# Context and attention in one block: the attention's tiles over the context's, its first loads issued during the eighth context block

## The chip, the core and the metric

The kernel runs on one core of a Trainium2 chip. The time is the device time of one execution in microseconds (us); a kernel's time is the median of its runs. Engines are named as in the profile: PE is TensorE, ACT ScalarE, DVE VectorE, POOL GpSimd, and SP is SyncE, which here only issues DMA transfers.

## The reference, cut to what matters

Four cross-attention layers on the same stream `x` (8 x 512 tokens x 512 channels) against one context (8 x 77 x 1024). Layers 0 and 2 are of kind A, 1 and 3 of kind B.

```python
# layers 0 and 2 (16 heads of 64, own K/V heads, bias on a few context columns)
q = x @ Wq;  k = ctx @ Wk;  v = ctx @ Wv
logits = einsum('bhqd,bhkd->bhqk', q, k) * 64 ** -0.5 + col_bias
x = softmax(logits) @ v  -> (B, 512, 1024) @ Wo + bo + x
# layers 1 and 3 (16 heads of 32, 4 K/V heads, rms norm of x)
xn = x * rsqrt(mean(x * x) + eps) * norm_w
q = xn @ wq;  k = ctx @ wk;  v = ctx @ wv
x = x + softmax(q k / sqrt(32)) @ v @ wo
```

Keys and values depend on the context alone, so they can be computed for all four layers ahead of the attention. Each float32 product is formed from a high and a low part in three matmul passes (`three_passes`, lines 228 to 232).

## The kernel before

The program is two hardware blocks, one after the other, in each of which every engine has its own hand-written instruction list. At the end of a block all five engines meet in a barrier.

**The context block** (`context_block`) projects the context with nine pairs of weight blocks, j = 0 to 8 (`NJ`): eight pairs for layers 0 and 2, one for layers 1 and 3 together. For each j, PE makes the keys (four banks, 96 matmuls of 308 columns) and then the values (five groups of rows r = 0 to 4, banks 4 to 7 and again 4, 24 matmuls of 256 columns each). ACT copies each bank's high part out and DVE subtracts it to get the low part (`drain_keys`, `drain_values`); both also split the next weights (`split_weights`). SP issues for each j: the two loads of the weights of j + 1 into `kvw_raw` (line 329), four stores of `k_out` to the scratch `k_scr` (line 340) and two of `v_out` to `v_scr` (lines 345 and 347).

In the ninth pair (j = 8) there are no further context weights. In their place SP loads the attention's first batch of x into `kvw_raw` slot 0 (line 331), half of the first query weights `wqA` into slot 1 (line 333), and, after x has been split (`late_lo` at least 1), the other half into slot 0 again (line 335). ACT splits x (`split_late(0)`, line 389) as its last work of j = 7, ahead of all of its work for j = 8. It splits the two weight halves between the drains of keys and of values of j = 8. PE's values r = 4 use bank 4 a second time, and so wait until DVE has drained r = 0 (the wait on `v_lo` in `values`). SP's last instruction in the block waits until every store has landed.

**The attention block** (`attention_block`) runs 128 units (4 layers, 8 batches, 4 head groups) in a software pipeline of steps: queries of the next unit, scores of this one, transposes of the one before, values of the one two back, projections. At its start POOL clears `keys_s` and `vals_s`, and SP issues the first loads, in this order: keys of unit 0 (2 transfers), two pieces of weights into `stage`, three of x into `x_front`, keys of unit 1 (2), values of units 0 and 1 (16 small transfers, line 663), four of x into `x_back`. After them SP follows the steps. All transfers of the kernel are issued by SP, on one queue.

The tiles of the two blocks take SBUF in turn; what lasts over both (`w_s`, `x_s` and some constants) is in `Lasting`.

Of the kernel before, what the change touches and what calls it, by code (L numbers as in the profile page):

```python
# [13 lines left out]

# [12 lines left out]
P = 128  # L27
# [226 lines left out]
def context_block(nc, lasting, ctxT, kvw, k_scr, v_scr, k1_scr, v1_scr, x_in, wqA, boA, normB, masks, tokens,  # L254
# [5 lines left out]
    with ExitStack() as ctx:  # L260
# [6 lines left out]
        ctx_raw = sb("ctx_raw", [P, KC, ROWS], F32)  # L267
        ctx_s = sb("ctx_s", [P, 2, KC, ROWS], F32R)
        w_raw = sb("kvw_raw", [P, 2, PART], F32)
        k_out = sb("k_out", [P, 2, 2, ROWS], F32R)  # L270
        v_out = sb("v_out", [P, len(VROWS), 2, BLK], F32R)
        banks = [ctx.enter_context(nc.psum_tensor(f"ctx_bank{i}", [P, 512], F32)) for i in range(8)]

        w_A, x_s, ident, mean_w, mhalf = lasting.w_s, lasting.x_s, lasting.ident, lasting.mean_w, lasting.mhalf
        bias_s, bo, nw = lasting.bias_s, lasting.bo, lasting.nw
        w_s = w_A[:, 2:4]
        tok_i = sb("tok_i", [P, 8], I32)
        tok_f = sb("tok_f", [P, 2, 8], F32)

        mask_b = sb("mask_b", [P, 2, TILES], F32)  # L280
        iota_t = ctx_raw[:, 2, 0:CTX]
        cmp_t = [ctx_raw[:, 2, CTX * (1 + n):CTX * (2 + n)] for n in range(3)]

        ctx_loaded = [sem(f"ctx_loaded{n}") for n in range(KC // 2)]
        first_loaded = [sem(f"first_loaded{n}") for n in range(KC // 2)]
        first_hi, first_lo = sem("first_hi"), sem("first_lo")
        w_loaded = [sem("kw_loaded"), sem("vw_loaded")]
        ctx_hi, ctx_lo = sem("ctx_hi"), sem("ctx_lo")
        w_hi, w_lo = [sem("kw_hi"), sem("vw_hi")], [sem("kw_lo"), sem("vw_lo")]
        k_mm, v_mm = sem("k_mm"), sem("v_mm")  # L290
        k_hi, k_lo, v_hi, v_lo = sem("k_hi"), sem("k_lo"), sem("v_hi"), sem("v_lo")
        k_stored, v_stored = sem("k_stored"), sem("v_stored")
        consts, cleared, setup_loaded, chain = map(sem, ("consts", "setup_cleared", "setup_loaded", "dve_chain"))
        late_loaded = [sem("x_first"), sem("wq_first"), sem("wq_second")]
        late_hi, late_lo = sem("late_hi"), sem("late_lo")
        NV = len(VROWS)
        FULL = sum(r == P for r in VROWS)

        def late_parts(n):
            if n == 0:  # L300
                return [x_s[:, 0, h].rearrange("p k n -> p (k n)") for h in range(2)]
            return [w_A[:, n - 1, h] for h in range(2)]

        def keys_stored(j):
            return 64 * j

        def vals_stored(j):
            return 32 * j

        block = ctx.enter_context(nc.Block())  # L310

        @block.sync
        def _(sp):
            for k in range(0, KC, 2):
                sp.dma_start(w_raw[:, 0, BLK * k:BLK * (k + 2)], kvw[0][:, BLK * k:BLK * (k + 2)]).then_inc(first_loaded[k // 2], 16)
                sp.dma_start(ctx_raw[:, k:k + 2], ctxT[:, k:k + 2]).then_inc(ctx_loaded[k // 2], 16)
            sp.dma_start(w_raw[:, 1], kvw[1]).then_inc(w_loaded[1], 16)
            sp.dma_start(mask_b[:, :, :], masks).then_inc(setup_loaded, 16)
            sp.dma_start(tok_i[:, :], tokens[:, ::token_words].partition_broadcast(P)).then_inc(setup_loaded, 16)
            sp.dma_start(bo[:, :, :], boA).then_inc(setup_loaded, 16)  # L320
            sp.dma_start(nw[:, :, :], normB).then_inc(setup_loaded, 16)
            for j in range(NJ):
                for slot in range(2):
                    if j == 0 and slot == 0:
                        sp.wait_ge(first_lo, KC // 2)
                    else:
                        sp.wait_ge(w_lo[slot], j + slot)
                    if j + 1 < NJ:
                        sp.dma_start(w_raw[:, slot], kvw[2 * j + 2 + slot]).then_inc(w_loaded[slot], 16)
                    elif slot == 0:  # L330
                        sp.dma_start(w_raw[:, 0], x_in[0].rearrange("p k n -> p (k n)")).then_inc(late_loaded[0], 16)
                    else:
                        sp.dma_start(w_raw[:, 1], wqA[0, 0]).then_inc(late_loaded[1], 16)
                        sp.wait_ge(late_lo, 1)
                        sp.dma_start(w_raw[:, 0], wqA[0, 1]).then_inc(late_loaded[2], 16)
# [23 lines left out]
        def _(act):  # L359
# [11 lines left out]
            def drain_keys(n, j):  # L371
                m, h = n // 2, n % 2
                act.wait_ge(k_mm, 4 * j + n + 1)
                if n == 0 and j:
                    act.wait_ge(k_stored, keys_stored(j))
# [951 lines left out]
```

## Time and profile before

| | us |
|---|---|
| median of 3 runs (2130.8 to 2134.89) | 2132.19 |
| the profiled execution, whole | 2131.65 |
| its span in the trace | 2129.7 |
| PE busy | 2080.0 (98%) |
| DVE busy | 1361.5 (64%) |
| ACT busy | 927.0 (44%) |
| POOL busy | 690.4 (32%) |

A row of instructions has the start and the duration, the engine, the line, the operation, out<-in and how many were merged, and in brackets how long the engine had been idle and what ended that. SPq rows are DMA issues: their duration is that of issuing, and the landing of the data is shown apart. In a row of stretches, "PEclk" is the granted TensorE clock as a share of full speed (1.00 is the 2.4 GHz level, 0.50 the 1.2 GHz level), "DMA share" the mean busy share of the 16 DMA engines and "GB/s" what they moved. The share can come out a little over 1, as whole packets are counted where they start.

### The profile page before, as it was taken

The page shows a single profiled execution, that of the slowest core. Times are in us where ns is not written, and L with a number is a line of the kernel's source. Part 1 is how long each engine was busy: PE and PEld are TensorE (multiplying, and loading weights), DVE is VectorE, ACT ScalarE, POOL GpSimd, SP SyncE. Part 2 cuts the span into 40 slices and gives each one's busy share as a digit, 9 for nine tenths or more (in the row PEclk, how much of TensorE's full clock was granted, in tenths as well). Part 3 has the DMA queues.
Part 4 walks back from the last instruction along what each step waited for, and adds up shares of the span by engine and source line. Part 5 has one row for each costly group of instructions (what it writes and reads, how often), then busy time and mean ns, then how long its engine had stood idle before and what let it go on. Part 6 is the DMA issues. An engine that isn't in the chain of part 4 may idle for free.

```text
span 2129.7 us, 31554 instructions
## 1 busy us (share of the span) xinstructions
PE 2080.0 (98%) x11674; PEld 1795.4 (84%) x11674; DVE 1361.5 (64%) x2344; ACT 927.0 (44%) x1750; POOL 690.4 (32%) x646
## 2 busy tenths in 40 slices
PE   8999999999999998999999999999999989999998
PEld 8999978888888887788888888888888877888886
DVE  5333355765576556688888675557655765888885
ACT  3222243543354334555555453335433543555552
POOL 0000043312231245465454431223122434554441
PEclk9999999999999999999999999999999999999999
DMA  7777842222222222343333332212221222233322
GB/s 213 173 158 157 179 120 74 67 62 74 54 65 63 77 60 72 85 110 100 86 95 92 102 90 67 73 55 65 63 76 51 70 72 80 67 94 88 87 71 81
DMA packets 260729, 191.02 MB, mean 90 GB/s; under 512 B 195842, under 2 KB 198306, under 8 KB 258018
## 3 DMA queue, kind: packets, MB, share of 16 engines
q1 hardware_dynamic: 260578, 189.02, 34.0%
q8 instruction: 93, 1.52, 0.3%
q14 instruction: 58, 0.48, 0.1%
HBM read 132.66 MB, written 56.26 MB: 89 GB/s over the span
## 4 chain that ended last, share of the span: by engine, by line
PE 38%; issue 31%; POOL 12%; DVE 4%; ACT 1%; SPq 1%; DMA 0%; POOLq 0%; ACTq 0%; DVEq 0%
POOL prob L1197 6%; PE acc_bank L804 6%; PE acc_bank L230 4%; PE acc_bank L232 4%; PE acc_bank L231 4%; PE t_bank L787 4%; PE q_bank L769 3%; PE q_bank L773 3%; PE q_bank L771 3%; POOL x_s L1172 3%; POOL rest L1205 2%; PE s_bank L230 2%; PE s_bank L232 2%; PE s_bank L231 1%; DVE pT_s L1077 1%
## 5 line engine op out<-in xcount | busy, mean ns | idle before, releaser
L1197 POOL TENSOR_TENSOR prob<-prob,rinv 128x1232 f32<-128x1232 f32 x128 | 288.3, 2252 | 1034.9 <-DVE rinv L1092 1034.9
L804 PE MATMUL acc_bank<-pT_s,vals_s 128*128 128x512 f32 x1152 | 369.7, 417 | 0.0
L1055 DVE TENSOR_REDUCE mx<-s_bank 128x4 f32<-128x308 f32 x512 | 243.4, 475 | 187.9 <-PE s_bank L735 117.5
L969 ACT ACTIVATE q_s<-q_bank 128x512 fp32r<-128x512 f32 x192 | 114.8, 598 | 528.7 <-PE q_bank L773 523.6
L769 PE MATMUL q_bank<-x_s,w_s 128*128 128x512 f32 x768 | 320.5, 417 | 4.0 <-POOL w_s L1190 4.0
L773 PE MATMUL q_bank<-x_s,w_s 128*128 128x512 f32 x768 | 314.6, 410 | 0.0
L771 PE MATMUL q_bank<-x_s,w_s 128*128 128x512 f32 x768 | 314.1, 409 | 0.0
L230 PE MATMUL acc_bank<-o_s,w_s 128*128 128x512 f32 x752 | 304.4, 405 | 3.0 <-DVE o_s L1083 3.0
L232 PE MATMUL acc_bank<-o_s,w_s 128*128 128x512 f32 x752 | 298.0, 396 | 0.0
L231 PE MATMUL acc_bank<-o_s,w_s 128*128 128x512 f32 x752 | 297.6, 396 | 0.0
L960 ACT ACTIVATE prob<-prob,rstd 128x308 f32<-128x308 f32 x256 | 140.0, 552 | 288.4 <-DVE prob L1059 260.6
L1059 DVE TENSOR_TENSOR prob<-s_bank,mx 128x308 f32<-128x308 f32 x512 | 244.9, 478 | 26.8 <-DVE mx L1055 0.5
L804 PEld LDWEIGHTS acc_bank<-pT_s,vals_s 128*128 128x128 f32 x1152 | 214.5, 189 | 39.5
L1077 DVE TENSOR_TENSOR pT_s<-t_bank,pT_s 128x512 fp32r<-128x512 f32 x256 | 175.6, 686 | 89.1 <-ACT pT_s L974 89.1
L974 ACT ACTIVATE pT_s<-t_bank 128x512 fp32r<-128x512 f32 x384 | 222.1, 594 | 23.8 <-PE t_bank L787 23.8
L1106 DVE SCALAR_TENSOR_TENSOR x_back<-acc_bank,bo,x_back 128x512 f32<-128x512 f32 x64 | 48.0, 750 | 248.7 <-PE acc_bank L232 248.6
L1089 DVE TENSOR_REDUCE sums<-prob 128x16 f32<-128x1232 f32 x128 | 183.2, 1431 | 3.6 <-ACT prob L952 1.6
L230 PEld LDWEIGHTS acc_bank<-o_s,w_s 128*128 128x128 f32 x752 | 141.6, 188 | 35.7 <-DVE o_s L1083 4.8
L232 PEld LDWEIGHTS acc_bank<-o_s,w_s 128*128 128x128 f32 x752 | 141.6, 188 | 34.3
L231 PEld LDWEIGHTS acc_bank<-o_s,w_s 128*128 128x128 f32 x752 | 142.0, 189 | 31.2
L773 PEld LDWEIGHTS q_bank<-x_s,w_s 128*128 128x128 f32 x768 | 146.1, 190 | 22.8
L769 PEld LDWEIGHTS q_bank<-x_s,w_s 128*128 128x128 f32 x768 | 146.6, 191 | 19.6 <-POOL w_s L1190 4.3
(105 smaller groups left out, 4086.0 us busy)
## 6 DMA issues: line engine op xcount, KB each, us to landing
stream<-x_back SPq DMA_DIRECT2D x128, 256.0 KB, 2.6
x_front<-stream SPq DMA_DIRECT2D x96, 256.0 KB, 3.3
x_back<-stream SPq DMA_DIRECT2D x96, 256.0 KB, 3.9
kvw_raw<-kvw SPq DMA_DIRECT2D x17, 1024.0 KB, 8.6
k_scr<-k_out SPq DMA_DIRECT2D x36, 308.0 KB, 8.4
keys_s<-k_scr SPq DMA_DIRECT2D x128, 77.0 KB, 2.5
v_scr<-v_out SPq DMA_DIRECT2D x8, 1024.0 KB
x_back<-x_in SPq DMA_DIRECT2D x32, 256.0 KB, 4.1
```

The lines of the kernel that those rows point to most:

```text
L230: pe.matmul(out, weights[0], moving[0], start=start, stop=False)
L231: pe.matmul(out, weights[0], moving[1], start=False, stop=False)
L232: return pe.matmul(out, weights[1], moving[0], start=False, stop=stop)
L769: pe.matmul(out, w[0], x_now[0], start=k == 0, stop=False)
L771: pe.matmul(out, w[0], x_now[1], start=False, stop=False)
L773: mm = pe.matmul(out, w[1], x_now[0], start=False, stop=k == XC - 1)
L804: mm = pe.matmul(out, w, pT_s[:, part], start=i == mine[0] and part == 2 * n and w is v[0], stop=i == mine[-1] and w is terms[-1][0] and p ...
L974: act.activation(pT_s[:, 2 * n], t_bank[(3 * u + n) % 2][:, :], ACT.Copy).then_inc(t_hi, 1)
L1055: dve.tensor_reduce(top, scored, AX_X, ALU.max).then_inc(s_max, 1)
L1059: dve.tensor_tensor(prob[:, slot, t].rearrange("q (h n) -> q h n", h=GH), scored, top.unsqueeze(2).broadcast_to([P, GH, CTX]), ALU.subtrac ...
L1077: dve.tensor_tensor(pT_s[:, 2 * n + 1], t_bank[(3 * u + n) % 2][:, :], pT_s[:, 2 * n].bitcast(F32), ALU.subtract).then_inc(t_lo, 1)
L1197: pool.tensor_tensor(view, view, rinv[:, slot].unsqueeze(2).broadcast_to([P, TILES * GH, CTX]), ALU.mult).then_inc(p_norm, 1)
```

## The change

There is one block. `context_part` holds what was `context_block`: it sets up its tiles, gives back their SBUF and PSUM, and returns its five engine lists as functions (`sync`, `scalar`, `vector`, `gpsimd`, `tensor`). `whole_block` is the old `attention_block`, and each of its engines runs the context's list and then its own, with no barrier between. Its tiles lie over the context's: `vals_s`, `keys_s`, `x_front` and the small tiles over `ctx_raw`; `o_s`, `xsq`, `x_power` and `rest` over `ctx_s`; `q_s` over `kvw_raw`; `prob` over `k_out`; `pT_s` over `v_out`; `x_back` and `stage` over the small setup tiles and on free space. Waits on semaphores take the barrier's place.

The first loads become a function `begin()`, which SP calls at j = 7, the eighth pair, after the weight loads of that pair and before the stores of its keys and values. The order in `begin` is new too.

```diff
+    def sync(sp, begin):
...
+                if j + 1 < NJ:
+                    sp.dma_start(w_raw[:, slot], kvw[2 * j + 2 + slot]).then_inc(w_loaded[slot], 16)
...
+            if j == NJ - 2:
+                begin()
+            for m in range(2):
+                sp.wait_ge(k_lo, 4 * j + 2 * m + 2)
...
-            sp.wait_ge(k_stored, keys_stored(NJ))
-            sp.wait_ge(v_stored, vals_stored(NJ - 1) + 48 * PAIRS)
...
+    return Context(sync, scalar, vector, gpsimd, tensor, late_lo, k_lo, 4 * NJ, k_stored, v_stored, chain,
+                   links_in_setup, keys_stored(NJ), vals_stored(NJ - 1) + 48 * PAIRS, keys_stored(2),
+                   vals_stored(2))
...
-            sp.wait_ge(keys_zeroed, 2)
-            load_keys(0)
-            load_weights(0)
-            load_weights(1)
-            for k in range(RING):
-                load_front(1, k)
-            load_keys(1)
-            sp.wait_ge(vals_zeroed, 2)
-            load_vals(0)
-            load_vals(1)
-            for m in range(XC):
-                load_back(0, m)
+            def begin():
+                sp.wait_ge(context.k_stored, context.wide_keys)
+                sp.wait_ge(context.v_stored, context.wide_vals)
+                sp.wait_ge(keys_zeroed, 2)
+                load_keys(0)
+                load_keys(1)
+                sp.wait_ge(vals_zeroed, 2)
+                load_vals(0)
+                load_vals(1)
+                load_weights(0)
+                load_weights(1)
+                for k in range(RING):
+                    load_front(1, k)
+                for m in range(XC):
+                    load_back(0, m)
+
+            context.sync(sp, begin)
             for s in range(STEPS):
+                if s == 0:
+                    sp.wait_ge(context.k_stored, context.all_keys)
+                    sp.wait_ge(context.v_stored, context.all_vals)
...
+            context.tensor(pe)
+            pe.wait_ge(context.k_lo, context.all_drained)
+            pe.wait_ge(context.late_lo, 3)
...
             def split_t(u, n):
+                if u == 0 and n == 0:
+                    act.wait_ge(context.v_stored, context.all_vals)
...
+            context.scalar(act)
...
+            context.vector(dve)
             for _ in rest_q(0):
                 pass
+            dve.wait_ge(context.k_stored, context.all_keys)
...
+            context.gpsimd(pool)
+            pool.wait_ge(context.chain, context.chain_end)
```

SP before, from the weight loads of j = 7 to the second late load of `wqA` in j = 8:

```order
L329 DMA kvw_raw<-kvw 128x2048 [waits kw_lo]
L329 DMA kvw_raw<-kvw 128x2048 [waits vw_lo]
L340 DMA k_scr<-k_out 128x8x77 [waits k_lo]
L340 DMA k_scr<-k_out 128x8x77
L340 DMA k_scr<-k_out 128x8x77 [waits k_lo]
L340 DMA k_scr<-k_out 128x8x77
L345 DMA v_scr<-v_out 128x4x512 [waits v_lo]
L347 DMA v_scr<-v_out 104x512
L331 DMA kvw_raw<-x_in 128x2048 [waits kw_lo]
L333 DMA kvw_raw<-wqA 128x2048 [waits vw_lo]
L335 DMA kvw_raw<-wqA 128x2048 [waits late_lo]
```

SP before, at the junction (the last value stores of j = 8, into the scratch of layers 1 and 3; the end of the block, the first keys):

```order
L351 DMA v1_scr<-v_out 128x4x128 x2
L353 DMA v1_scr<-v_out 208x1x128
L260 UNCONDITIONAL_BRANCH [waits v_stored,k_stored]
L618 UNCONDITIONAL_BRANCH [waits barrier_Pool_Activation_PE_DVE_SP_release]
L644 DMA keys_s<-k_scr 64x4x77 [waits keys_zeroed]
L644 DMA keys_s<-k_scr 64x4x77
```

The first loads stand behind the block's end and its barrier, and the stores of j = 7 (the first four `k_scr` rows) directly behind the weight loads.

SP now, from the weight loads of j = 7 on (keys of two units, then the first of 16 value loads):

```order
L336 DMA kvw_raw<-kvw 128x2048 [waits kw_lo]
L336 DMA kvw_raw<-kvw 128x2048 [waits vw_lo]
L659 DMA keys_s<-k_scr 64x4x77 [waits keys_zeroed,v_stored,k_stored]
L659 DMA keys_s<-k_scr 64x4x77
L659 DMA keys_s<-k_scr 64x4x77 [waits keys_zeroed]
L659 DMA keys_s<-k_scr 64x4x77
L678 DMA vals_s<-v_scr 77x2x64 [waits vals_zeroed]
L678 DMA vals_s<-v_scr 51x2x64
L678 DMA vals_s<-v_scr 26x2x64
L678 DMA vals_s<-v_scr 26x64
```

SP now, from the last of the value loads to the late load of x in j = 8:

```order
L678 DMA vals_s<-v_scr 26x64
L687 DMA stage<-woA 128x512 x2
L643 DMA x_front<-x_in 128x512 x3
L649 DMA x_back<-x_in 128x512 x4
L349 DMA k_scr<-k_out 128x8x77 [waits k_lo]
L349 DMA k_scr<-k_out 128x8x77
L349 DMA k_scr<-k_out 128x8x77 [waits k_lo]
L349 DMA k_scr<-k_out 128x8x77
L354 DMA v_scr<-v_out 128x4x512 [waits v_lo]
L356 DMA v_scr<-v_out 104x512
L338 DMA kvw_raw<-x_in 128x2048 [waits kw_lo]
L340 DMA kvw_raw<-wqA 128x2048 [waits vw_lo]
```

29 transfers (4 of keys, 16 of values, 2, 3 and 4 of 256 KB) have come between the weight loads and the key stores of j = 7, and with that ahead of the load `kvw_raw<-x_in` of j = 8.

PE before, from its last context matmuls (values r = 4 of j = 8, bank 4) to its first of the attention:

```order
L230 MATMUL ctx_bank4<-w_s,ctx_s 104x256
L231 MATMUL ctx_bank4<-w_s,ctx_s 104x256
L232 MATMUL ctx_bank4<-w_s,ctx_s 104x256
L260 UNCONDITIONAL_BRANCH
L716 UNCONDITIONAL_BRANCH [waits barrier_Pool_Activation_PE_DVE_SP_release]
L864 MATMUL s_bank0<-x_s 128x308
L864 MATMUL s_bank1<-x_s 128x308
```

PE now, at the same place:

```order
L231 MATMUL ctx_bank4<-w_s,ctx_s 104x256
L232 MATMUL ctx_bank4<-w_s,ctx_s 104x256
L233 MATMUL ctx_bank4<-w_s,ctx_s 104x256
L890 MATMUL s_bank0<-x_s 128x308 [waits late_lo,k_lo]
L890 MATMUL s_bank1<-x_s 128x308
```

The block's end and the barrier have gone, and two waits on DVE's drains (`k_lo`, `late_lo`) stand before the first matmul.

## Rows read from the trace of the kernel before

**Rows 1.** Timeline of PE around the junction (columns as told above).

```profile
261.86 0.28 PE L232 MATMUL ctx_bank<-w_s,ctx_s 128*104 128x256 f32 x1
269.62 0.85 PE L864 MATMUL s_bank<-x_s 128*128 128x308 f32 x2 [7.49 <-PEq L260]
```

**Rows 2.** Stretches after the junction: busy per engine, PEclk, DMA share, GB/s.

```profile
266.00:268.00 2.00, 0.00 (x0) 0.00 (x0) 0.00 (x0) 0.00 (x0) 0.00 (x0) 0.69 1.01 298
270.00:272.00 2.00, 2.00 (x7) 1.61 (x7) 0.00 (x0) 0.78 (x2) 2.00 (x4) 0.50 0.00 0
272.00:274.00 2.00, 2.00 (x7) 1.61 (x6) 0.00 (x0) 0.00 (x0) 0.53 (x1) 0.60 0.59 152
274.00:276.00 2.00, 2.00 (x11) 1.62 (x10) 0.60 (x1) 0.60 (x1) 0.00 (x0) 1.00 0.96 265
276.00:278.00 2.00, 2.00 (x12) 1.67 (x11) 0.09 (x1) 0.49 (x1) 0.00 (x0) 1.00 0.87 252
```

**Rows 3.** Chain of the critical path: the same matmul at either clock level.

```profile
270.90 0.43 PE q_bank L771
274.27 0.23 PE q_bank L771
```

**Rows 4.** Timeline of SP: its issues in j = 7 and j = 8.

```profile
208.30 3.08 SPq L329 DMA_DIRECT2D kvw_raw<-kvw  x2
214.28 9.17 SPq L340 DMA_DIRECT2D k_scr<-k_out  x4
235.18 0.36 SPq L345 DMA_DIRECT2D v_scr<-v_out  x1
236.49 0.43 SPq L331 DMA_DIRECT2D kvw_raw<-x_in  x1
248.65 0.33 SPq L335 DMA_DIRECT2D kvw_raw<-wqA  x1
249.42 6.63 SPq L340 DMA_DIRECT2D k_scr<-k_out  x4
263.04 0.91 SPq L351 DMA_DIRECT2D v_scr<-v_out  x2
...
266.18 0.85 SPq L353 DMA_DIRECT2D v_scr<-v_out  x1
```

**Rows 5.** Stretches of j = 7 and the start of j = 8.

```profile
214.00:217.00 3.00, 3.00 (x23) 3.00 (x23) 0.25 (x1) 0.28 (x1) 0.00 (x0) 1.00 1.02 410
217.00:220.00 3.00, 3.00 (x23) 3.00 (x22) 0.48 (x1) 0.15 (x1) 0.00 (x0) 1.00 1.14 264
220.00:222.00 2.00, 2.00 (x19) 2.00 (x18) 0.48 (x1) 1.87 (x2) 0.00 (x0) 1.00 0.76 75
225.00:228.00 3.00, 3.00 (x28) 3.00 (x27) 0.43 (x2) 0.39 (x1) 0.00 (x0) 1.00 0.98 71
228.00:235.00 7.00, 7.00 (x61) 7.00 (x60) 1.12 (x3) 1.47 (x4) 0.00 (x0) 1.00 0.02 3
235.00:236.00 1.00, 1.00 (x9) 1.00 (x9) 0.15 (x1) 1.00 (x1) 0.00 (x0) 1.00 0.00 0
236.00:239.00 3.00, 3.00 (x23) 3.00 (x22) 2.29 (x1) 0.49 (x1) 0.00 (x0) 1.00 1.01 345
```

**Rows 6.** Timelines of ACT, then DVE, in j = 8.

```profile
244.38 1.92 ACT L389 ACTIVATE x_s<-kvw_raw 128x2048 fp32r<-128x2048 f32 x1 [7.88 <-DMA kvw_raw<-x_in]
254.43 1.92 ACT L389 ACTIVATE w_s<-kvw_raw 128x2048 fp32r<-128x2048 f32 x1 [4.27 <-DMA kvw_raw<-wqA]
...
246.33 2.29 DVE L435 TENSOR_TENSOR x_s<-kvw_raw,x_s 128x2048 fp32r<-128x2048 f32 x1 [7.51 <-ACT x_s L389]
256.38 2.29 DVE L435 TENSOR_TENSOR w_s<-kvw_raw,w_s 128x2048 fp32r<-128x2048 f32 x1 [3.89 <-ACT w_s L389]
258.58 1.53 DVE L429 TENSOR_TENSOR v_out<-ctx_bank,v_out 128x256 fp32r<-128x256 f32 x4
```

**Rows 7.** Timeline of PE at the start of values r = 4 of j = 8.

```profile
258.96 0.27 PE L232 MATMUL ctx_bank<-w_s,ctx_s 128*128 128x256 f32 x1
259.08 0.35 PE L230 MATMUL ctx_bank<-w_s,ctx_s 128*104 128x256 f32 x1
```

**Rows 8.** Timeline of SP: the first loads of the attention.

```profile
270.77 1.28 SPq L644 DMA_DIRECT2D keys_s<-k_scr  x2
272.08 1.07 SPq L672 DMA_DIRECT2D stage<-woA  x2
273.20 1.38 SPq L628 DMA_DIRECT2D x_front<-x_in  x3
274.62 1.18 SPq L644 DMA_DIRECT2D keys_s<-k_scr  x2
275.92 12.50 SPq L663 DMA_DIRECT2D vals_s<-v_scr  x16
288.47 1.79 SPq L634 DMA_DIRECT2D x_back<-x_in  x4
```

**Rows 9.** Waits of POOL up to 300 us (us in total, times, longest); ACT's timeline.

```profile
POOL keys_s L1218 <- POOLq L260: 251.1, 1, 251.1
...
297.42 0.58 ACT L974 ACTIVATE pT_s<-t_bank 128x512 fp32r<-128x512 f32 x1
```

**Rows 10.** DMA issues, 264 to 300 us: count, KB each, median us to landing.

```profile
x_back<-x_in SPq DMA_DIRECT2D x4, 256.0 KB, 3.8
keys_s<-k_scr SPq DMA_DIRECT2D x8, 77.0 KB, 3.2
...
vals_s<-v_scr SPq DMA_DIRECT2D x4, 38.5 KB
vals_s<-v_scr SPq DMA_DIRECT2D x4, 25.5 KB
vals_s<-v_scr SPq DMA_DIRECT2D x4, 13.0 KB
vals_s<-v_scr SPq DMA_DIRECT2D x4, 6.5 KB
```

**Rows 11.** Stretches at the loads of `x_back` (issued from 288.47).

```profile
288.50:289.50 1.00, 1.00 (x5) 0.81 (x4) 0.35 (x1) 1.00 (x2) 1.00 (x2) 0.50 0.21 28
289.50:293.00 3.50, 3.50 (x18) 2.96 (x17) 2.30 (x4) 1.19 (x4) 2.80 (x2) 0.83 0.91 293
```

More of the change, by code:

```diff
@@ L15 @@
+from collections import namedtuple
 from contextlib import ExitStack
@@ L251, in __init__, with context_part @@
         self.nw = sb("nw", [P, PAIRS, XC], F32)
-def context_block(nc, lasting, ctxT, kvw, k_scr, v_scr, k1_scr, v1_scr, x_in, wqA, boA, normB, masks, tokens,
+Context = namedtuple("Context", "sync scalar vector gpsimd tensor late_lo k_lo all_drained k_stored v_stored chain chain_end "
+                                "all_keys all_vals wide_keys wide_vals")
+def context_part(nc, ctx, lasting, ctxT, kvw, k_scr, v_scr, k1_scr, v1_scr, x_in, wqA, boA, normB, masks, tokens,
                   token_words):
@@ new lines, in context_part @@
+    first_hi, first_lo = sem("first_hi"), sem("first_lo")
+    w_loaded = [sem("kw_loaded"), sem("vw_loaded")]
+    ctx_hi, ctx_lo = sem("ctx_hi"), sem("ctx_lo")
+    w_hi, w_lo = [sem("kw_hi"), sem("vw_hi")], [sem("kw_lo"), sem("vw_lo")]
+    k_mm, v_mm = sem("k_mm"), sem("v_mm")
+    k_hi, k_lo, v_hi, v_lo = sem("k_hi"), sem("k_lo"), sem("v_hi"), sem("v_lo")
+    k_stored, v_stored = sem("k_stored"), sem("v_stored")
+    consts, cleared, setup_loaded, chain = map(sem, ("consts", "setup_cleared", "setup_loaded", "dve_chain"))
@@ new lines, in scalar, with split_weights, drain_keys, drain_values @@
+    def scalar(act):
+        def split_weights(slot, j):
+            if j:
+                act.wait_ge(w_loaded[slot], 16 * (j + slot))
+                if slot == 0:
+                    act.wait_ge(k_mm, 4 * j)
+                else:
+                    act.wait_ge(v_mm, NV * j)
+            else:
+                act.wait_ge(w_loaded[slot], 16)
+            act.activation(w_s[:, slot, 0], w_raw[:, slot], ACT.Copy).then_inc(w_hi[slot], 1)
+        def drain_keys(n, j):
+            m, h = n // 2, n % 2
+            act.wait_ge(k_mm, 4 * j + n + 1)
+            if n == 0 and j:
+                act.wait_ge(k_stored, keys_stored(j))
+            act.activation(k_out[:, m, 0, h * HALF:(h + 1) * HALF], banks[n][:, 0:HALF], ACT.Copy)\
+               .then_inc(k_hi, 1)
+        def drain_values(r, j):
+            act.wait_ge(v_mm, NV * j + r + 1)
+            if r == 0 and j:
+                act.wait_ge(v_stored, vals_stored(j))
+            act.activation(v_out[0:VROWS[r], r, 0], banks[4 + r % 4][0:VROWS[r], 0:BLK], ACT.Copy)\
+               .then_inc(v_hi, 1)
+        def split_late(n):
+            act.wait_ge(late_loaded[n], 16)
+            act.activation(late_parts(n)[0], w_raw[:, n % 2], ACT.Copy).then_inc(late_hi, 1)
+        for k in range(KC):
+            if k % 2 == 0:
+                act.wait_ge(first_loaded[k // 2], 16)
+                act.activation(w_s[:, 0, 0, BLK * k:BLK * (k + 2)], w_raw[:, 0, BLK * k:BLK * (k + 2)], ACT.Copy).then_inc(first_hi, 1)
+            act.wait_ge(ctx_loaded[k // 2], 16)
+            act.activation(ctx_s[:, 0, k], ctx_raw[:, k], ACT.Copy).then_inc(ctx_hi, 1)
+        split_weights(1, 0)
+        for j in range(NJ):
+            for n in range(4):
+                drain_keys(n, j)
+            if j + 1 < NJ:
+                split_weights(0, j + 1)
+            else:
+                split_late(1)
+                split_late(2)
+            for r in range(NV):
+                drain_values(r, j)
+            if j + 1 < NJ:
+                split_weights(1, j + 1)
+            if j + 2 == NJ:
+                split_late(0)
@@ L287, in context_block @@
[L287 to L308, printed above, removed]
```

460 lines of the change are left out of this document (208 added, 252 removed).

## The prediction

> **What bounds the kernel now.** The page comes first: PE is busy for 2080.0 of 2129.7 us, so the change can only give back what PE loses around the junction of the two blocks. The timeline of PE shows that place [rows 1]: the last context matmul starts at 261.86 and is through at 262.14, the first of the attention starts at 269.62. That is 7.48 us in which PE has nothing. SP spends the first 5 of them on the last value stores [rows 4], and the block's end waits for their landing. A second loss is in the table of stretches [rows 2]: the granted clock falls during the pause, to the 1.2 GHz level (0.50), and is back at 1.00 after 274. The chain of the critical path has the price of it [rows 3]: 0.43 us for a matmul of 512 columns at the lower level, 0.23 us at the full one. From 269.62 to about 273.6 PE so did in 4.0 us what takes 2.0 us: 2.0 us lost. Pause and clock together are 9.5 us, 0.45% of the kernel. No more can be won here.
>
> Next I looked at who sets the pace inside the eighth and ninth pairs (j = 7 and 8). SP's timeline has the issues [rows 4], the stretches say when the DMA engines are full [rows 5]: share 1.02, 1.14 and 0.98 between 214 and 228, 0.02 from 228 to 235, nothing from 235 to 236, and 1.01 from 236 on. There is one hole of about 8 us in j = 7, and the first loads will be put ahead of it or into it. In j = 8 ACT stands still for 7.88 us until the first x lands, at 244.38 [rows 6]. From there a chain runs without slack: ACT splits x (to 246.3), DVE makes its low part (to 248.62), SP issues the second half of `wqA` at 248.65 [rows 4], it lands at 254.43, ACT splits it, DVE makes its low part from 256.38 to 258.67 and drains values r = 0 from 258.58, the first of four drains in 1.53 us, so until about 259.0 [rows 6]. PE's values r = 4 wait for just that drain, and start at 259.08, 0.12 us after the matmul ahead of them [rows 7]. The last 24 context matmuls therefore hang on the landing of x with a slack of about 0.1 us. Before, this costs nothing, because it fits by a hair.
>
> **The change part by part.**
>
> Removed: the block's end, the barrier and SP's wait for the stores. PE then goes from values r = 4 straight on. The new waits of PE (`late_lo` 3, `k_lo`) are for drains that DVE issues ahead of the drain of r = 0, and cost nothing. Gain 7.48 us, as long as values r = 4 still end at 262.14.
>
> Moved with it: the stores of j = 8 now overlap the attention. Their waits come later: DVE asks for the key stores ahead of its first scores, SP for all stores at step 0, ACT for the value stores at its first transposes. In the old trace SP has issued the last of them by 267.03 [rows 4], and they had landed when the barrier opened, before 269.62 [rows 1]; ACT's first transposes come 28 us after that, at 297.42 [rows 9]. Even if the stores move 10 us to the right, these waits are covered: 0. POOL's clearings of `keys_s` and `vals_s` move ahead, into the 251.1 us in which POOL had nothing to do [rows 9]: 0. Laying tiles over one another issues nothing: 0.
>
> Moved: 29 loads on SP's queue, ahead of four key stores, two value stores and the load of x. This is the term that decides. `begin` starts behind the second weight load, at 208.30 + 3.08 = 211.38 [rows 4]. Issue times are those of the same transfers after the junction [rows 8]: keys 1.28 + 1.18, values 12.50, which makes 226.4 with the gaps between them; then weights 1.07, x_front 1.38, x_back 1.79, which makes 230.6. Key stores were issued from 214.28 on; now they can't be before 230.6, 16 us later.
>
> What the DMA engines do in that time: they are full until about 218 with the weights of j = 8. From there to 226.4 they get only keys and values, 0.64 MB (four of 77 KB, and 4 times 38.5 + 25.5 + 13 + 6.5 KB) [rows 10] in small pieces spread over 15 us of issuing, so most of this time passes nearly idle, where before they worked on key stores. The hole of 8 us has been moved ahead and not filled. The first data of a 256 KB load come about 1.1 us after its issue: `x_back` is issued at 288.47, and the share is 0.21 up to 289.5 and 0.91 from there [rows 11]. So the nine big loads of 256 KB [rows 10], 2.36 MB, start to move at 227.5; at the 293 GB/s of the same form of load [rows 11] they take 8.05 us, until 235.5. The key stores behind them took the engines from 217 to 228, with a dip to 0.76 where SP came with the second pair only at 221 [rows 5]; I take 10.0 us without the dip: 245.5. Then come the value stores and x. Before, their data moved from 236.0 on [rows 5] and x landed at 244.38 [rows 6], 8.4 us later. Now x lands at 245.5 + 8.4 = 253.9, that is 9.5 us late. SP itself reaches the issue of x in time: in j = 8 before, four key stores took it 6.63 us [rows 4], so from 230.6 it is done by about 238 and with the value stores by 239, well ahead of 245.
>
> The sum: the chain from x to values r = 4 has only the durations told above and an otherwise idle queue, so it moves as it is. Values r = 4 start at 259.08 + 9.5 = 268.6 and end at 271.6. The attention starts there, where it started at 269.62: +2.0 us. The barrier's pause of 7.48 us gives way to a pause of 9.5 us one group of matmuls earlier. A pause of that length let the clock fall before, so I leave its cost at the same 2.0 us: 0. The profiled execution was 2131.65, the median 2132.19; on the median this gives **2134.2 us**.
>
> Bounds of the uncertain terms. The big loads: 2.36 MB at the 252 GB/s that the table shows from 276 to 278 [rows 2] is 9.4 us (+1.3); at 345 GB/s, as from 236 to 239 [rows 5], 6.8 us (-1.2). The key stores: 9 to 11 us (-1 to +1). The clock: the 24 matmuls of r = 4 may now run at the lower level as well, 3 us more at most, of which I'd see 1.5; or it recovers earlier, 2 us less.
>
> The Trainium skill, DMA: Bandwidth & Descriptors, Specifications, gives about 358 GB/s for one core's HBM traffic. By that figure, as an estimate, the nine loads would take 6.6 us and the sum would come to +0.6 us. The trace's 293 GB/s for this very form of load decides for me. The same page, Queues, rings and completion order, says that each DMA engine takes its descriptors in ring order. By that rule x can't pass the key stores; the trace agrees so far as x, issued 236.49, landed 7.9 us later behind value stores issued at 235.2. Its section Two DMAs through the same engine are not ordered says that a later one may finish first; that is the rival A below.
>
> **The rivals.**
>
> A, faster: x does not wait for the whole backlog. If the engines work on several transfers at once, x needs after its issue what it needed before, 7.9 us [rows 4, 6]. It is issued at about 239.5, where SP gets to it, and lands at 247.4: 3.0 us late. Then the pause shrinks from 7.48 to 3.0 us, and may be too short for the clock to fall: -4.5 to -6.5 us, 2125.7 to 2127.7. With no delay at all it is the full -9.5: 2122.7. For it: the second half of `wqA` took only 5.8 us on a free queue. Against: the share is at 1 when it matters, so someone has to wait.
>
> B, slower: the backlog is dearer. SP pushes 29 loads ahead of the key stores; with the big loads at 252 GB/s and key stores at 12 us, one more than all the time from 217 to 228 [rows 5], x lands at 236.9 + 12 + 8.4 = 257.3, 12.9 us late. With values r = 4 at the lower clock, +1.5: 12.9 - 7.5 + 1.5 = +6.9 us, 2139.1. It decides from the point where x lands after 256.2.
>
> C, no effect by construction: that the new waits for `k_stored` and `v_stored` act as a barrier again. They would have to come more than 10 us later than reckoned, and PE has 24 query matmuls and four score groups ahead of them. It gives at most what the barrier cost, the same time as before; I count it with the forecast.
>
> **How the numbers follow.** Forecast, with C: 0.60, from -4.3 to +4.3 us of the old median, 2127.9 to 2136.5, with 2134.2 in its upper half. A: 0.18. B: 0.22. About 0.2%, 4.3 us, is what a measurement of this kernel can tell from no change. So faster by more 0.18, within it 0.60, slower by more 0.22. The range for 8 in 10 goes from 2126.5 (into A) to 2139.0 (to the end of B).
>
> **What would show it.** In the profile after: no pause of PE between values r = 4 and the matmuls into `s_bank`; in its place a pause ahead of values r = 4, some 9 us from 259.1 on, put down to DVE's `v_out` drain. ACT's wait for the first x grows from 7.9 to some 17 us, until 254. Key stores of j = 7 are issued from 230.6, and the DMA share is low from 219 to 227 and full from 228 to past 250. If x lands before 248, A holds and the engines do not work in order; if it lands after 256, B. If PE's pause before the attention is still there, C.

## The result

| | before | after |
|---|---|---|
| median, us (20 runs each) | 2131.98 (2130.8 to 2134.89) | 2134.77 (2133.68 to 2138.33) |
| the profiled execution, whole | 2131.65 | 2133.91 |
| its span in the trace | 2129.7 | 2132.0 |
| PE busy | 2080.0 | 2076.7 |

The ratio is 1.0015, with a 95% interval of 1.0008 to 1.0021: slower by 2.8 us, within 0.2% of before. The forecast was 2134.2 us.

The pause before the attention has gone, and a longer one stands ahead of values r = 4. In the timeline of PE after, the last matmul ahead of the pause, the first after it, and the first of the attention (the columns are those of [rows 1]):

```profile
258.88 0.27 PE L233 MATMUL ctx_bank<-w_s,ctx_s 128*128 128x256 f32 x1
272.19 0.54 PE L231 MATMUL ctx_bank<-w_s,ctx_s 128*104 128x256 f32 x1 [13.03 <-DVE v_out L434]
...
276.91 0.45 PE L890 MATMUL s_bank<-x_s 128*128 128x308 f32 x2
```

In [rows 7] the first matmul of r = 4 followed its predecessor after 0.12 us. Now it comes 13.1 us late (PE idle for 13.0 us), and the attention starts at 276.91 where it started at 269.62 [rows 1]: +7.3 us, against +2.0 in the forecast. Of this, 2.0 us are only borrowed: before, PE paid for the lower clock behind that point, and now ahead of it, in r = 4 itself, which takes 4.72 us (272.19 to 276.91) instead of 3.06 (259.08 to 262.14), 1.7 more. So the sum is +13.1 for the new pause, -7.5 for the old one, +1.7 and -2.0 for the clock: +5.3 us.

Where the pause comes from stands in the timelines of ACT and DVE in j = 8, to be read beside [rows 6]:

```profile
257.13 1.92 ACT L395 ACTIVATE x_s<-kvw_raw 128x2048 fp32r<-128x2048 f32 x1 [20.71 <-DMA kvw_raw<-x_in]
...
267.56 1.91 ACT L395 ACTIVATE w_s<-kvw_raw 128x2048 fp32r<-128x2048 f32 x1 [5.46 <-DMA kvw_raw<-wqA]
...
259.08 2.29 DVE L440 TENSOR_TENSOR x_s<-kvw_raw,x_s 128x2048 fp32r<-128x2048 f32 x1 [20.34 <-ACT x_s L395]
...
269.51 2.29 DVE L440 TENSOR_TENSOR w_s<-kvw_raw,w_s 128x2048 fp32r<-128x2048 f32 x1 [4.39 <-ACT w_s L395]
271.71 1.41 DVE L434 TENSOR_TENSOR v_out<-ctx_bank,v_out 128x256 fp32r<-128x256 f32 x4
```

x lands at 257.13 where it landed at 244.38, 12.75 us later. The rest of the chain moves with it: the second half of `wqA` lands at 267.56 (254.43 before, +13.1), and DVE's drain of values starts at 271.71 (258.58 before, +13.1).

SP's timeline shows what stands ahead of x; the rows answer to [rows 4] and [rows 8]:

```profile
211.48 2.65 SPq L659 DMA_DIRECT2D keys_s<-k_scr  x4
214.66 13.16 SPq L678 DMA_DIRECT2D vals_s<-v_scr  x16
227.87 0.84 SPq L687 DMA_DIRECT2D stage<-woA  x2
228.75 1.38 SPq L643 DMA_DIRECT2D x_front<-x_in  x3
230.18 2.33 SPq L649 DMA_DIRECT2D x_back<-x_in  x4
232.55 8.07 SPq L349 DMA_DIRECT2D k_scr<-k_out  x4
240.66 3.59 SPq L354 DMA_DIRECT2D v_scr<-v_out  x1
244.30 1.36 SPq L356 DMA_DIRECT2D v_scr<-v_out  x1
245.70 1.15 SPq L338 DMA_DIRECT2D kvw_raw<-x_in  x1
...
261.40 0.33 SPq L342 DMA_DIRECT2D kvw_raw<-wqA  x1
```

And the stretches, with the columns of [rows 5] (PEclk, DMA share and GB/s are the last three):

```profile
220.00:222.00 2.00, 2.00 (x20) 2.00 (x18) 0.48 (x1) 1.96 (x2) 0.00 (x0) 1.00 0.25 55
222.00:225.00 3.00, 3.00 (x28) 3.00 (x27) 2.63 (x2) 0.66 (x2) 0.00 (x0) 1.00 0.12 27
225.00:228.00 3.00, 3.00 (x27) 3.00 (x27) 0.42 (x1) 0.39 (x1) 0.00 (x0) 1.00 0.12 28
228.00:231.00 3.00, 3.00 (x28) 3.00 (x27) 0.43 (x1) 0.39 (x1) 0.00 (x0) 1.00 0.61 181
231.00:235.00 4.00, 4.00 (x35) 4.00 (x34) 0.78 (x2) 1.16 (x3) 0.00 (x0) 1.00 0.86 242
...
239.00:242.00 3.00, 3.00 (x24) 3.00 (x23) 0.00 (x0) 0.00 (x0) 0.00 (x0) 1.00 1.37 112
242.00:246.00 4.00, 4.00 (x30) 4.00 (x30) 0.00 (x0) 0.00 (x0) 0.00 (x0) 1.00 1.41 93
...
254.00:258.00 4.00, 4.00 (x36) 4.00 (x35) 0.00 (x0) 0.87 (x1) 0.00 (x0) 1.00 0.95 395
```

From 220 to 228 the DMA engines are at 0.25 and 0.12: SP is busy issuing small value loads, which give them next to nothing to do. [Rows 5] had key stores there. From 229 on the share is high, and stays so until x has landed (254 to 258 is nearly all data of x and of the first half of `wqA` behind it, at 395 GB/s). Where the key stores move in pieces of 308 bytes the share is counted up to 1.41, well over 1; it is to be read as full. The idle stretch that stood at 228 to 236 has been moved ahead to 220 to 228; nothing has been hidden in it.

The junction so accounts for +5.3 us, but the spans differ by 2.3. I therefore compared the start of each PE matmul, all 11674, after with before. From the junction on the distance falls slowly. Taking only differences of up to 0.06 us between neighbours, so that no wait and no change of clock is counted, the attention from 300 us on is 2.34 us faster after than before, and the context 0.00: the same matmuls follow one another a little faster. The larger differences (24 waits and changes of clock) sum to -0.75. With 5.3 - 2.3 - 0.75 = +2.3 the spans agree. The middle term isn't in the forecast at all.

### The profile page after: what moved, and what is told of

It is laid out like the page before. It is cut to its first block, busy times and chain, and to the rows that moved or that the text cites. A ratio compares the mean times of both kernels' runs of the same rounds, so it can differ in the third digit from the quotient of the medians.

```text
span 2132.0 us, 31546 instructions
## 1 busy us (share of the span) xinstructions
PE 2076.7 (97%) x11674; PEld 1793.0 (84%) x11674; DVE 1361.9 (64%) x2344; ACT 927.0 (43%) x1750; POOL 691.5 (32%) x646
## 4 chain that ended last, share of the span: by engine, by line
PE 46%; issue 31%; POOL 12%; DVE 5%; SPq 2%; DMA 2%; ACT 2%; POOLq 0%; ACTq 0%; DVEq 0%
POOL prob L1228 6%; PE acc_bank L827 6%; PE acc_bank L231 4%; PE acc_bank L233 4%; PE acc_bank L232 4%; PE t_bank L810 4%; PE q_bank L796 3%; PE q_bank L792 3%; PE q_bank L794 3%; POOL x_s L1203 3%; PE ctx_bank L231 3%; PE ctx_bank L232 3%; PE ctx_bank L233 3%; POOL rest L1236 2%; PE s_bank L231 2%
## 5 line engine op out<-in xcount | busy, mean ns | idle before, releaser
L1002 ACT ACTIVATE pT_s<-t_bank 128x512 fp32r<-128x512 f32 x384 | 222.1, 594 | 23.8 <-PE t_bank L810 23.8
## 6 DMA issues: line engine op xcount, KB each, us to landing
k_scr<-k_out SPq DMA_DIRECT2D x36, 308.0 KB, 10.2
```

The source lines that it names most:

```text
L1002: act.activation(pT_s[:, 2 * n], t_bank[(3 * u + n) % 2][:, :], ACT.Copy).then_inc(t_hi, 1)
```

## The experiments

**The theory**: x waits for all that is ahead of it on SP's one queue. The 20 small loads hurt by the time SP takes to issue them, in which the DMA engines have little work; the nine large ones by their bytes. **The rivals**: the loads aren't the cause, but the missing barrier (the stores of j = 8 and other work that now overlaps); or the large loads alone are, since they are most of the bytes. And a second question, where the 2.3 us in the attention come from: the new addresses of the tiles, or the new overlap.

Each ratio is to the kernel before, run beside it on the same chip (medians 2132.36 for e1 to e4, 2132.05 for e5, e6 and f1; the last three are single runs next to a single one of 2130.66, so their traces count and not their times). E1 has nine runs, e2, e6 and f1 eleven each, e3, e4 and e5 five each. The first six change the changed kernel, the others the kernel before.

| experiment | median, us | ratio, 95% interval | x split at | PE's pause at r = 4 |
|---|---|---|---|---|
| after | 2134.77 | 1.0015 (1.0008 to 1.0021) | 257.13 | 13.0 |
| `e1_begin_last` | 2127.36 | 0.9975 (0.9966 to 0.9985) | 244.49 | 0.2 |
| `e2_big_behind_keys` | 2134.41 | 1.0007 (0.9998 to 1.0016) | 256.98 | 12.7 |
| `e3_small_in_j6` | 2123.25 | 0.9954 (0.9940 to 0.9968) | 248.19 | 5.6 |
| `e4_in_the_holes` | 2119.14 | 0.9936 (0.9924 to 0.9949) | 244.90 | 0.7 |
| `e5_begin_in_j6` | 2123.10 | 0.9958 (0.9945 to 0.9970) | 246.86 | 1.6 |
| `e6_x_ahead_of_keys` | 2128.87 | 0.9986 (0.9977 to 0.9995) | 241.62 | 7.8 |
| `f1_layout_alone` | 2130.06 | 0.9992 (0.9983 to 1.0002) | 244.46 | none; barrier |
| `g1_keys_in_one_go` | 2131.22 | one run | | |
| `f2_shift_512` | 2130.91 | one run | | |
| `f3_order_without_gap` | 2128.26 | one run | | |

**e1_begin_last**: one block, the first loads behind the whole context.

```diff
-            if j == NJ - 2:
-                begin()
...
             context.sync(sp, begin)
+            begin()
```

> One block, but the 29 first loads are issued only after the whole of the context's SP list, where the old kernel has them; no barrier. Backlog theory: the load of x of j = 8 lands at about 244.4 us again (12.7 us earlier than in the changed kernel), ACT waits 7.9 us for it, PE has no pause before values r = 4 and none before the attention: 7.5 + 2.0 us less than before, 2122.5 us. Rival (the merged block itself costs: stores under the attention, new waits on k_stored and v_stored): the time stays at 2132 us or above.

x lands as before and the pause at r = 4 is gone, so it is the loads, and not the missing barrier, that delay x. The time is 5 us more than I expected. The waits of PE from 200 to 300 us (in total, times, longest) show why, and the stretches show the clock:

```profile
PE s_bank L751 <- DMA keys_s<-k_scr: 2.6, 1, 2.6
...
270.00:272.00 2.00, 1.15 (x3) 1.04 (x4) 0.00 (x0) 0.00 (x0) 0.00 (x0) 0.59 0.49 105
272.00:274.00 2.00, 2.00 (x7) 1.65 (x6) 0.00 (x0) 0.00 (x0) 0.00 (x0) 0.50 0.15 34
```

SP gets to the first keys at 267.59 only, behind the value stores of j = 8, and PE waits 2.6 us for them. The clock falls at 270.4 and stays at 0.50 until 277.2, with work. Compared start by start, PE was 9.2 us ahead of the kernel before when it came to this wait, and 5.7 of them were lost again by 292 us. So the loads do have to come earlier than the end of the context.

**e2_big_behind_keys**: the small loads as in the changed kernel, the nine large ones behind the key stores of j = 7.

```diff
             if j == NJ - 2:
-                begin()
+                small()
             for m in range(2):
                 sp.wait_ge(k_lo, 4 * j + 2 * m + 2)
...
+            if j == NJ - 2:
+                large()
             sp.wait_ge(v_lo, NV * j + NV)
```

> As changed, but the nine loads of 256 KB go behind the key stores of j = 7; the 20 small ones stay ahead of them. Backlog theory: the sum of the work ahead of x is the same and only its order differs, so x still lands at 254 to 257 us and the time is 2133 to 2135 us. Rival (what hurts is that the key stores are held back by the big loads, through SP being held at the fourth store): x lands 4 us or more earlier and the time falls under 2130 us.

x is split at 256.98, within 0.2 us of the changed kernel. The order of large loads and key stores among themselves made no difference here, only that both are ahead of x.

**e3_small_in_j6**: the 20 small loads ahead of the stores of j = 6, the large ones left where they are.

```diff
+            if j == NJ - 3:
+                small()
             if j == NJ - 2:
-                begin()
+                large()
```

> As changed, but the 20 small loads (15.8 us of issuing) go one pair earlier, ahead of the stores of j = 6. Backlog theory: the DMA engines are not left idle from 220 to 228 in j = 7, j = 6 leaves a backlog of some 3 us: x lands at about 249 us, 8 us earlier than in the changed kernel, 4.6 us later than before; the time is 2127 us. Rival (the nine big loads are what costs): x lands at 254 or later, 2132 us or more.

x comes 8.9 us earlier than in the changed kernel, and 3.8 us later than before. So moving the 20 small loads, which have a fifth of the bytes (0.64 of 3.0 MB), one pair ahead takes away 8.9 of the 12.75 us. The 3.8 that stay aren't the large loads' alone: the weights of j = 8 land at 221.9 and 225.4, 5.2 and 5.7 us later than before (216.7, 219.7), so part of what the small loads left behind in j = 6 is in them, and this run doesn't part the two. The time is 3.8 us under the expected one, which left out the 2.2 us that this kernel's matmuls, too, are closer. ACT's timeline has what is left of the delay; the second half of `wqA` came 1.9 us slower than in the changed kernel (7.31 against 5.46 of idle time):

```profile
248.19 1.92 ACT L397 ACTIVATE x_s<-kvw_raw 128x2048 fp32r<-128x2048 f32 x1 [11.45 <-DMA kvw_raw<-x_in]
...
260.49 1.91 ACT L397 ACTIVATE w_s<-kvw_raw 128x2048 fp32r<-128x2048 f32 x1 [7.31 <-DMA kvw_raw<-wqA]
```

**e4_in_the_holes**: each part of the first loads directly *behind* the key stores of a pair, where SP would wait for the values: keys and values of unit 0 in j = 5, values of unit 1 in j = 6, the large ones in j = 7.

```diff
-            if j == NJ - 2:
-                begin()
             for m in range(2):
                 sp.wait_ge(k_lo, 4 * j + 2 * m + 2)
...
+            if j in (NJ - 4, NJ - 3):
+                small(j - (NJ - 4))
+            if j == NJ - 2:
+                large()
             sp.wait_ge(v_lo, NV * j + NV)
```

> The loads are spread behind the key stores of three pairs, where both SP and the DMA engines have a hole: keys and values of unit 0 in j = 5, values of unit 1 in j = 6, the nine big ones in j = 7. Backlog theory: x lands at 244.4 to 246 us, no pause of PE before values r = 4 over 1.5 us: 2122.5 to 2124 us, as with the loads last. Rival (any load ahead of x costs its own transfer time): x lands 8 us late, 2130 us or more.

This is the fastest of all, by 0.64% (0.51 to 0.76%) against the kernel before, and 3.4 us under the lower end of what was expected. First SP's timeline, then one of the stretches, then ACT's timeline and PE's waits from 200 to 300 us:

```profile
214.10 7.80 SPq L347 DMA_DIRECT2D k_scr<-k_out  x4
221.94 2.50 SPq L689 DMA_DIRECT2D stage<-woA  x2
224.49 1.75 SPq L645 DMA_DIRECT2D x_front<-x_in  x3
226.28 7.16 SPq L651 DMA_DIRECT2D x_back<-x_in  x4
234.99 0.38 SPq L356 DMA_DIRECT2D v_scr<-v_out  x1
...
230.00:234.00 4.00, 4.00 (x36) 4.00 (x35) 0.42 (x1) 0.39 (x1) 0.00 (x0) 1.00 0.99 220
...
244.90 1.92 ACT L397 ACTIVATE x_s<-kvw_raw 128x2048 fp32r<-128x2048 f32 x1 [8.59 <-DMA kvw_raw<-x_in]
...
PE ctx_bank L231 <- DVE v_out L436: 0.7, 1, 0.7
```

The key stores are issued at 214.1, as before, and most of the large loads move in the stretch that was idle before (share 0.99 from 230 to 234, where [rows 5] have 0.02). SP is through with them at 233.4, before the value stores are due at 235, and x is split only 0.5 us later than before. PE has no pause that lets the clock fall at the junction. Against the trace before, PE's matmuls run 8.9 us ahead after the junction (7.5 + 2.0 less the 0.7, within 0.1); 1.6 us more come from a fall of the clock that the kernel before has at 287 to 291, the changed one at 293 to 297, and this one not; 2.6 us from the closer matmuls. Together 13.1; the medians differ by 13.2, the spans by 14.0. The 1.6 us can't be put down to where the loads stand: g1 and f2, which issue the first loads as the kernel before does, lack that fall too.

**e5_begin_in_j6**: all of `begin` one pair earlier.

```diff
-            if j == NJ - 2:
+            if j == NJ - 3:
                 begin()
```

> As changed, but begin() is called one pair earlier, at j = 6, with the same 29 loads in the same order. Backlog theory: the same 9 to 13 us of backlog now falls on the weight loads of j = 8, which PE needs only at 234 us, and the 8 us hole of j = 7 takes up most of it: x lands 1 to 5 us late, the time is 2118 to 2126 us. Rival (begin costs SP and the DMA engines the same wherever it stands in the context): PE waits 9 us or more in the next pair, 2132 us or more.

The same backlog now falls on j = 7, and ACT's timeline shows it there:

```profile
222.72 1.39 ACT L382 ACTIVATE k_out<-ctx_bank 128x308 fp32r<-128x308 f32 x4 [14.19 <-DMA k_scr<-k_out]
227.71 1.92 ACT L375 ACTIVATE w_s<-kvw_raw 128x2048 fp32r<-128x2048 f32 x1 [3.60 <-DMA kvw_raw<-kvw]
```

But j = 7 has slack: ACT catches up, and x is split at 246.86, 2.5 us late. PE waits 2.7 us in two pieces, 1.1 ahead of values r = 4 of j = 7 and 1.6 ahead of those of j = 8, and the clock stays at 1.00 until 281.6. With the same loads in the same order, one pair earlier, the kernel is 11.7 us faster than the changed one. What they cost is set by what stands behind them.

**e6_x_ahead_of_keys**: the load of x directly behind `begin`, ahead of the key stores.

```diff
             if j == NJ - 2:
                 begin()
+                sp.wait_ge(w_lo[0], j + 1)
+                sp.dma_start(w_raw[:, 0], x_in[0].rearrange("p k n -> p (k n)")).then_inc(late_loaded[0], 16)
```

> As changed, but the load of x for j = 8 goes directly behind begin, ahead of the key stores of j = 7. If the DMA engines take SP's transfers in order: x lands at about 241 to 243 us instead of 257, ACT's wait for it ends there; the key and value stores now stand ahead of the first half of wqA alone, which lands at about 257, and DVE's low part of x at 245 lets SP issue the second half of wqA directly behind the first, so that it lands at about 259: PE's pause before values r = 4 shrinks from 13 us to 4 or 5 us, 2122 to 2126 us. Rival (transfers in flight share the engines, so their order matters little): x lands at 250 us or later, the time stays within 2 us of the changed kernel's.

x is there at 241.62, 2.8 us earlier than before, so it did wait for the stores and not for something else. The pause is 7.8 us and not the 4 to 5 that I had reckoned with. ACT's timeline, from the split of x to that of the second half of `wqA`:

```profile
241.62 1.92 ACT L395 ACTIVATE x_s<-kvw_raw 128x2048 fp32r<-128x2048 f32 x1 [4.98 <-DMA kvw_raw<-x_in]
253.99 1.39 ACT L382 ACTIVATE k_out<-ctx_bank 128x308 fp32r<-128x308 f32 x4 [10.45 <-DMA k_scr<-k_out]
259.50 1.91 ACT L395 ACTIVATE w_s<-kvw_raw 128x2048 fp32r<-128x2048 f32 x1 [4.13 <-DMA kvw_raw<-wqA]
262.56 1.91 ACT L395 ACTIVATE w_s<-kvw_raw 128x2048 fp32r<-128x2048 f32 x1 [1.15 <-DMA kvw_raw<-wqA]
```

The two halves of `wqA`, now last behind the backlog, are split at 259.50 and 262.56, where 257 and 259 had been expected. The second, by way of DVE, sets the end of the pause at 267.19. ACT waits elsewhere too: its drains of j = 8 write `k_out`, which the key stores of j = 7 still have to read, and those have become late. That wait isn't what PE pays for, since ACT, done with the drains, stands idle for another 4.13 us until the first half of `wqA` is there. Whatever is put behind the backlog has something that waits for it. After, e2 and e6 together show that data comes in the order of the queue (x is split at 257.13 and 256.98 behind the key stores, at 241.62 ahead of them). The Trainium skill, DMA: Bandwidth & Descriptors, Queues, rings and completion order, says that each DMA engine consumes descriptors in ring order, and these three runs agree, though the same passage leaves open that a later one completes first.

**g1_keys_in_one_go**: the kernel before, with all four key stores of j = 7 issued together, as the backlog makes SP do it.

```diff
-                    sp.wait_ge(k_lo, 4 * j + 2 * m + 2)
+                    sp.wait_ge(k_lo, 4 * j + (4 if j == NJ - 2 else 2 * m + 2))
```

> The kernel before, but the key stores of j = 7 are all issued after the last key drain, behind one another, as they stand in the changed kernel. If key stores are dearer when four are queued at once (11.6 us of data in the changed kernel against the 10.0 of the prediction), their data take 11.5 us or more here too, from about 222 to 234, and the fourth lands 13 us after its issue; if their speed only scatters from pair to pair, 10 to 11 us. The time stays at 2132 us either way, since x is loaded after 236.

This was to explain why the data of the key stores took 11.6 us in the changed kernel (237.0 to 248.6, from the first hundredth to the last of the packets of 308 bytes) and not 10 (10.2 in the kernel before, 217.4 to 227.7, in the same measure). Here they took 9.4 us (222.1 to 231.5), so queuing four at once isn't dearer. Over the kernels the duration in j = 7 ranges from 9.4 to 12.0 us. The earlier pairs, in which nothing has been moved, say more. In the trace of the changed kernel the stores of the five pairs between 78 and 190 us take 11.3 to 12.0 us, in that of the kernel before 9.9 to 11.1. So the stores were slower in that whole execution, long before `begin`, and the backlog isn't the cause. The runs go together by chip: in those five pairs e1 and e2 (one chip) take 10.6 to 11.5 us, e6, f1 and the last three (two other chips) 9.3 to 11.2. Whether it is the chip, and what on it, wasn't tested, and the chip of the two kernels compared in the result isn't known.

**f1_layout_alone**: the kernel before, two blocks and its barrier, with the attention's tiles in the order of the changed kernel (and its gap of 512 bytes). Next to it **f2_shift_512**, the old order behind 512 unused bytes, and **f3_order_without_gap**, the new order without the gap.

```diff
+        vals_s = sb("vals_s", [P, 2, 4, 2, P], F32R)
+        keys_s = sb("keys_s", [P, 2, 2 * SC], F32R)
         x_front = sb("x_front", [P, RING, TOK], F32)
-        x_back = sb("x_back", [P, XC, TOK], F32)
-        q_s = sb("q_s", [P, 2, 2, 2, TOK], F32R)
...
+        o_s = sb("o_s", [P, 2, 8, TOK], F32R)
+        xsq = sb("xsq", [P, TOK], F32)
+        x_power = sb("x_power", [P, TOK], F32)
+        rest = sb("rest", [P, TILES, P], F32)
+        sb("unused", [P, 128], F32)
+
+        q_s = sb("q_s", [P, 2, 2, 2, TOK], F32R)
+        prob = sb("prob", [P, 2, TILES, SC], F32)
+        pT_s = sb("pT_s", [P, 5, TOK], F32R)
+
+        x_back = sb("x_back", [P, XC, TOK], F32)
+        stage = sb("stage", [P, 2, QUARTER], F32)
```

> The kernel before, two blocks and its order of loads, with only the attention's tiles in the order, and so at the SBUF addresses, of the changed kernel. If the addresses are what makes PE 2.3 us faster over the attention in all kernels with one block (sum of the differences of at most 20 ns between the starts of matmuls), the same 2.3 us show here and the time is 2129.8 us. If it is anything else (the missing barrier, where the code lies), the matmuls keep the old spacing within 0.3 us in sum and the time is 2132 us.

> The kernel before with 512 unused bytes per partition ahead of the attention's tiles, so that every one of them lies 512 bytes further on and their order is the old one. If any shift makes the matmuls closer, the sum of the small differences is about -2.3 us again; if the order of the tiles does it, it is 0 within 0.3 us.

> The kernel before with the attention's tiles in the changed kernel's order, but without the unused 512 bytes in it, so that q_s, prob, pT_s, x_back and stage lie 512 bytes lower. If the order is what counts, the sum of the small differences is -2.3 us within 0.5; if the exact place of those five does, it is another.

The sums of the small differences (up to 0.06 us) against the kernel before, over the attention's matmuls from 300 us on, are -2.36 us in f1 (-2.34 in the changed kernel), -0.20 in f2 and -2.82 in f3. With the 20 ns of the expectation they are -2.4 (-2.5), -0.3 and -2.6. G1, with the old tiles, gives -0.10 and is the measure of what this comparison makes of nothing. The other kernels with the new order give -2.2 to -2.6, but e5 only -1.5, for which I have no cause. So the gain is there in full without the overlap, from the layout alone; and it is the order of the tiles, not a shift of all. The median of f1 is 2.0 us below the kernel before, with an interval that just includes 1. The groups of PE by line, from 320 us on (busy, mean ns of one, idle before), first of the kernel before, then of the changed one, of f1 and of f2:

```profile
L232 PE MATMUL acc_bank<-o_s,w_s 128*128 128x512 f32 x752 | 298.0, 396 | 0.0
```

```profile
L233 PE MATMUL acc_bank<-o_s,w_s 128*128 128x512 f32 x752 | 296.9, 395 | 0.0
```

```profile
L232 PE MATMUL acc_bank<-o_s,w_s 128*128 128x512 f32 x752 | 296.9, 395 | 0.0
```

```profile
L232 PE MATMUL acc_bank<-o_s,w_s 128*128 128x512 f32 x752 | 298.1, 396 | 0.0
```

It is the same pass of the projection each time: 1.1 us less in 752 matmuls with the new order, nothing with the shift alone. Which tile, or which pair of them, does it wasn't separated. Matmuls of `q_bank<-x_s,w_s` come closer too, about 2 ns from the last pass of one to the first of the next (0.25 in f2 and g1), and neither of their operands has moved, so it can't be their own operands' address alone.

## Why the prediction was right, and where it was not

The time came out 0.6 us from the forecast, inside its range. The mechanism was right; that the number is so near is luck. The delay of x came out 3.2 us too large for the forecast and a gain that it put at nothing took 2.3 back, and on the way one of its own thresholds was passed.

- **The mechanism** (the new waits cost nothing, the pause moves ahead of values r = 4, x decides it by way of the second `wqA` and DVE's drain): as forecast. E1 and e4 give the counterproof: with x in time the pause is all but gone (0.2 and 0.7 us).
- **The start of the stores**: SP was through with `begin` at 232.55 and not 230.6. The 16 value loads took 13.16 us where I took the 12.50 of [rows 8]; from the first key load to the first value load it was 3.18 and not 2.5; the nine large ones took 4.6 for 4.2. The data of the key stores began to move at 237.0 and not 235.5: 1.5 us of the miss. SP itself came to the load of x at 245.70 and not at 239, as the four key stores held it for 8.07 us and the value stores for 4.95. That cost nothing, as the value stores ahead of x still moved until about 253, but the forecast had SP there "well ahead". The 358 GB/s that the prediction also reckons with is passed in these traces: 395 from 254 to 258 here, 410 in [rows 5].
- **The mis-sized term**: the key stores. I took 10.0 us, with 9 to 11 as bounds; they measured 11.6. That is 1.6 us more of the miss, and outside the bounds I gave. I had read the number from one pair in one trace; over the runs it scatters from 9.4 to 12.0, and the profiled execution of the changed kernel had slow stores from its start (g1).
- **From the value stores to x**: 8.5 us against 8.4. Right. So x came 12.75 us late, not 9.5, and PE's pause was 13.0 us.
- **The clock**: the level was low for longer, 262.6 to 276.2, but most of that fell into the pause. PE worked at it for 4.0 us (272.19 to 276.2), as before, and it cost 1.7 us against 2.0. That is the 0 that I had assumed, within 0.3; the extra 1.5 of rival B for r = 4 did not come, since r = 4 took over what the queries had paid before.
- **What was missing**: the tiles' addresses. "Laying tiles over one another issues nothing: 0" is true of instructions and false of time: -2.3 us. With it my own sum would have been -0.3 and not +2.0.
- **The balance** against my sum of +2.0: +3.6 for the later values r = 4 (3.2 of them by x, the rest by the second half of `wqA`), -0.3 for the clock, -2.3 for the addresses, and -0.75 for waits and short falls of the clock later in the attention, each of which moves by up to 1.7 us from trace to trace and which I can't put down to the change. That makes +2.3 for the profiled executions; the medians give +2.8.
- **Rival B** had put its threshold at x landing after 256.2. x landed at 257.13, so by the landing B held, and by the time it didn't: its 2139.1 counted 1.5 us for the clock that didn't come, and missed the 2.3 us as the forecast did. Had I known when x lands, my time would have been further off. **Rival A** is out: x landed 11.4 us after its issue and not 7.9, so it didn't pass the backlog, and e6 shows it gains when it is put ahead. **Rival C** is out: PE doesn't wait at `s_bank` before the attention.

## What to carry to other kernels

A transfer issued early on an in-order queue is paid for by whatever stands behind it. So look first for the transfer without slack (here x, 0.1 us), and for the stretches in which both the issuing engine and the DMA engines have nothing to do, and put the loads right behind the stores that precede those stretches, no more than fit into each: the same loads made a pause of 13.0 us all together ahead of the stores of j = 7, and of 0.7 us when they stood behind the stores of three pairs (e4). Which of the two counts for more, standing behind the stores or being spread, wasn't tested. All 29 behind the stores of j = 7 would not fit: SP took 21.1 us for them (211.48 to 232.55), and in e4 it has 13.0 between the key stores and the value stores. Count small transfers by the time of their issue, not by their bytes: moving 20 of them, with a fifth of the bytes, one pair ahead took away 8.9 of 12.75 us of delay. A forecast that comes true can stand on errors that cancel; compare the positions of a few landmarks in both traces, not the totals only.

## What the runs showed of the hardware

- The order of tiles in SBUF changes how closely matmuls follow each other, by up to about 2 ns at 512 columns, in matmuls whose own operands haven't moved too. Over the attention this makes 2.2 to 2.8 us in eight of the nine kernels with the new order and 1.5 in e5, against 0.2 with a plain shift by 512 bytes (f2) and 0.1 with the old tiles (g1).
- Issuing holds SP up when stores queue: four key stores issued in a row took SP 3.21 us on an idle queue (g1), 8.07 us behind the large loads (after) and 12.10 us in e3. The 9.17 us of [rows 4] don't belong here: 5.8 of them are the wait for the second pair of drains.
- The same four key stores, 1.26 MB in pieces of 308 bytes, move in 9.4 to 12.0 us, slower or faster by the execution or the chip (g1); full DMA engines then carry only 93 to 112 GB/s (after, 239 to 246), where they carry 395 GB/s with the load of x.
- The granted clock also falls without a long pause. In e1 it falls at 270.4, within a pause of PE of 2.6 us, and in the kernel before at 287.2, after pauses of 0.41 and 0.84 us; it is back at 1.00 at 277.2 and at 290.7.
